# Output projection of eight row tiles: three of four partial products formed inside the attention loop and added to x by GpSimd

## The reference, cut to what matters

```python
def _L1_ffn_ref(x, pos_w, pos_b, qkv_w, qkv_b, wo_w, wo_b):      # HEADS 8, TOPK 16
    pos = lax.conv_general_dilated(...)                           # three taps along the rows
    x = x + (pos + pos_b[None, :, None]).transpose(0, 2, 1)
    qkv = x @ qkv_w.T + qkv_b
    q, k, v = jnp.split(qkv, [c, 2 * c], axis=-1)                 # then split into 8 heads of 64
    logits = jnp.einsum('bmd,bpd->bmp', qd * scale, kd)
    _, idx = lax.top_k(logits, TOPK)
    ...
    attn = jax.nn.softmax(jnp.einsum('bmd,bmkd->bmk', q * scale, k_sel), axis=-1)
    out = jnp.einsum('bmk,bmkd->bmd', attn, v_sel)
    ...
    return out @ wo_w.T + wo_b

x = x + _L1_ffn_ref(_layernorm(x, axis=-1)[None], ...)[0]
```

## Time and profile before

| | |
|---|---|
| median of 3 runs | 1774.48 us (1774.18 to 1774.99) |
| the profiled execution, own time | 1774.77 us |
| its span | 1772.1 us |
| TensorE matmuls busy | 1527.8 us, 86% |
| VectorE busy | 1062.0 us, 60% |
| ScalarE busy | 699.6 us, 39% |
| GpSimd busy | 525.6 us, 30% |
| mean granted TensorE clock | 0.965 of full speed |
| loop of the 80 turns (first maximum to last striking out) | 1234.7 to 1724.6 us |

### The profile page before, as it was taken

The page is one execution under the profiler, slowest core; times in us unless marked ns, Lnnn a source line. Parts: engine busy times, 40 slices in busy tenths (PEclk is TensorE's granted clock), DMA queues, the critical chain, the costliest instruction groups (busy, mean ns, idle before and its releaser), DMA issues. The chain is left out here.

```text
span 1772.1 us, 22747 instructions
## 1 busy us (share of the span) xinstructions
PE 1527.8 (86%) x8385; PEld 940.5 (53%) x8385; DVE 1062.0 (60%) x2052; ACT 699.6 (39%) x1333; POOL 525.6 (30%) x388
## 2 busy tenths in 40 slices
PE   1885888789787788999999989958898999998878
PEld 0332544344466665445454654535586676776654
DVE  4998433333478774111322331574999999999991
ACT  0224000133365554110111132042778778878771
POOL 0001100000456651000000006001876766676550
PEclk9998899899899999999999999989999999999999
DMA  6000100000622212300000020002011011111001
GB/s 220 1 1 1 74 0 0 0 1 1 179 60 43 48 31 86 132 0 0 1 0 0 1 72 0 0 1 60 1 31 31 1 31 31 23 32 31 1 1 58
DMA packets 28570, 56.99 MB, mean 32 GB/s; under 512 B 7904, under 2 KB 12644, under 8 KB 28208
## 3 DMA queue, kind: packets, MB, share of 16 engines
q1 hardware_dynamic: 27600, 54.01, 11.0%
q10 hardware_dynamic: 864, 1.57, 0.3%
HBM read 28.77 MB, written 5.84 MB: 20 GB/s over the span
## 5 line engine op out<-in xcount | busy, mean ns | idle before, releaser
L1431 POOL TENSOR_TENSOR tl_ex<-tl_ex,tl_left 128x1250 f32<-128x1250 f32 x80 | 209.8, 2622 | 37.3 <-ACT tl_left L1733 33.2
L1552 PE MATMUL tl_banks<-identf,tl_ex 128*128 128x128 f32 x800 | 139.4, 290 | 42.2 <-ACT tl_pt L1754 25.7
L1272 DVE SCALAR_TENSOR_TENSOR X<-ex_ps_x,g,X 128x512 f32<-128x512 f32 x80 | 59.9, 750 | 192.6 <-PE ex_ps_x L1165 192.6
L1138 PE MATMUL ex_ps_h<-yt,w 128*128 128x512 f32 (+1 forms) x384 | 144.5, 531 | 0.0
L1165 PE MATMUL ex_ps_x<-w,hid 128*128 128x512 f32 (+1 forms) x320 | 143.1, 599 | 0.0
L1552 PEld LDWEIGHTS tl_banks<-identf,tl_ex 128*128 128x128 f32 x800 | 90.0, 144 | 97.4 <-ACT tl_pt L1754 44.4
L1754 ACT COPY tl_pt<-tl_banks 128x512 f32<-128x512 f32 (+1 forms) x200 | 108.4, 542 | 83.5 <-PE tl_banks L1552 79.7
L1218 ACT ACTIVATE hid<-ex_ps_h,b 128x512 f32<-128x512 f32 (+1 forms) x48 | 29.2, 610 | 242.6 <-PE ex_ps_h L1138 242.6
L1829 DVE MAX8 tl_m<-tl_banks 128x8 f32<-128x1250 f32 x80 | 116.3, 1454 | 5.6 <-PE tl_banks L1529 5.6
L1733 ACT ACTIVATE tl_left<-tl_left,tl_negm 128x1250 f32<-128x1250 f32 x80 | 107.6, 1345 | 29.0 <-DVE tl_left L1837 28.6
L1835 DVE MAX8 tl_m<-tl_left 128x8 f32<-128x1250 f32 x80 | 117.1, 1464 | 2.8
(11 more groups left out here) (268 smaller groups left out, 2963.8 us busy)
## 6 DMA issues: line engine op xcount, KB each, us to landing
kl<-KT SPq DMA_DIRECT2D x16, 320.0 KB, 4.4
qs<-QO SPq DMA_DIRECT2D x16, 320.0 KB, 5.8
tl_kl<-tl_KT SPq DMA_DIRECT2D x16, 320.0 KB, 4.4
tl_qs<-tl_QO SPq DMA_DIRECT2D x16, 320.0 KB, 6.0
w<-in_L_ffn_W SPq DMA_DIRECT2D x8, 512.0 KB
w<-in_L_ffn_W SPq DMA_DIRECT2D x4, 1024.0 KB, 9.8
at_kept<-AT SPq DMA_DIRECT2D x1, 3200.0 KB, 9.0
AT<-at_kept SPq DMA_DIRECT2D x1, 3200.0 KB, 18.9
```

The lines of the kernel that those rows point to most:

```text
L1138: mm = pe.matmul(h_bank(u)[:, 0:w], w1[e][:, k, j * P:(j + 1) * P], yt[:, G % 2, k, 0:w], start=(k == 0), stop=(k == KD - 1))
L1431: pool.tensor_tensor(ex[:, n % EXS, 0:N], ex[:, n % EXS, 0:N], left[:, n % LEFT, :], ALU.subtract).then_inc(s_probs, 1)
L1552: mm = pe.transpose(ps_t[:, b * P:(b + 1) * P], ex[:, n % EXS, a + b * P:a + (b + 1) * P], m.identf[:, :])
```

## The change

The three first column blocks of QO are complete once the first six heads are done (turn 59, normalised by turn 63). For the first EARLY = 8 row tiles their three products with `wo` are formed as jobs `out` at turns 65, 67, ... 79, one row tile each; ScalarE copies the result into a new buffer `partial`, and GpSimd adds it to x two turns later. `project(t)` of these tiles then forms the product of the last block alone. So that `wo` is there in time, its transposes move from turns 61 to 67 to turns 57 to 63, and the raw weight is loaded at the start of the loop, by four DMAs, into four vectors (`bias0`, `bias1`, `gamma1`, `beta1`) that no one reads any more, since the old place was still in use.

```diff
+    EARLY = 8
     for b in range(KD):
-        work_at[61 + 2 * b] = ("wo", b, None)
+        work_at[57 + 2 * b] = ("wo", b, None)
+    for t in range(EARLY):
+        work_at[65 + 2 * t] = ("out", t, None)
...
-    qkv_jobs = jobs_before[61]
+    qkv_jobs = jobs_before[57]
...
-        raw_wo = space("tl_raw_wo", 40960, [P, KD, D])
+        raw_wo = (m.bias0, m.bias1, m.gamma1, m.beta1)
+        partial = space("tl_partial", 40960, [P, EARLY, D])
...
-                    if (i, half) == (3, 0):
-                        sp.wait_ge(s_job, qkv_jobs)
-                        sp.dma_start(raw_wo[:, :, :], rows_of(io["L1_ffn_wo_w"])).then_inc(s_wo_in, 16)
+                    if (i, half) == (0, 1):
+                        for b in range(KD):
+                            sp.dma_start(raw_wo[b][:, :], io["L1_ffn_wo_w"][b * P:(b + 1) * P, :]).then_inc(s_wo_in, 16)
...
+                if n - 2 in work_at and work_at[n - 2][0] == "out":
+                    t = work_at[n - 2][1]
+                    pool.wait_ge(s_job_kept, kept_after[n - 2])
+                    pool.tensor_tensor(m.X[:, t, :], m.X[:, t, :], partial[:, t, :], ALU.add).then_inc(s_added, 1)
+                    pool.wait_ge(s_added, t + 1)
...
+                    if kind == "out":
+                        pe.wait_ge(s_normed, (2 * HP - 3) * NT // 2 + i // 2 + 1)
...
+                    if part >= HP - 1:
+                        return
+                    mm = pe.matmul(ps_o, QO[:, part, i * P:(i + 1) * P], wo[:, part, :], start=(part == 0),
+                                   stop=(part == HP - 2))
...
-                for k in range(KD):
-                    mm = pe.matmul(proj_bank(t), QO[:, k, t * P:(t + 1) * P], wo[:, k, :], start=(k == 0),
+                ks = range(HP - 1, KD) if t < EARLY else range(KD)
+                for k in ks:
+                    mm = pe.matmul(proj_bank(t), QO[:, k, t * P:(t + 1) * P], wo[:, k, :], start=(k == ks[0]),
                                    stop=(k == KD - 1))
...
+                elif kind == "out":
+                    act.copy(partial[:, i, :], ps_o).then_inc(s_job_kept, 1)
                 else:
+                    act.wait_ge(s_job, qkv_jobs)
                     act.copy(wo[:, :, i * P:(i + 1) * P], ps_o.rearrange("p (k c) -> p k c", k=KD)
...
                 dve.wait_ge(s_biased, t + 1)
+                if t < EARLY:
+                    dve.wait_ge(s_added, t + 1)
                 dve.wait_ge(s_projected, t + 1)
```

More of the change, by code:

```diff
@@ L1321, in top_layer @@
         (s_zn, s_w_turned, s_w_kept, s_x_turned, s_x_kept, s_edge, s_tapped, s_mid, s_conv, s_first, s_first_kept,
-         s_job, s_job_kept, s_wo_in, s_staged_k,
+         s_job, s_job_kept, s_wo_in, s_added, s_staged_k,
          s_fetched_0, s_fetched_1, s_staged, s_scored, s_max, s_negm, s_read, s_max2, s_topped, s_exp, s_rest,
@@ L1325, in top_layer @@
          s_projected, s_final, s_stored) = s.signals(
-            "zn w_turned w_kept x_turned x_kept edge tapped mid conv first first_kept job job_kept wo_in staged_k "
+            "zn w_turned w_kept x_turned x_kept edge tapped mid conv first first_kept job job_kept wo_in added staged_k "
             "fetched_0 fetched_1 staged scored max negm read max2 topped exp rest sum inv blank probs turned kept "
@@ L1384, in _ @@
                                          ).then_inc(s_fetched[half], 16)
-                    if (i, half) == (3, 0):
-                        sp.wait_ge(s_job, qkv_jobs)
-                        sp.dma_start(raw_wo[:, :, :], rows_of(io["L1_ffn_wo_w"])).then_inc(s_wo_in, 16)
+                    if (i, half) == (0, 1):
+                        for b in range(KD):
+                            sp.dma_start(raw_wo[b][:, :], io["L1_ffn_wo_w"][b * P:(b + 1) * P, :]).then_inc(s_wo_in, 16)
             for half in range(2):
                 sp.wait_ge(s_fetched[half], 64 * HP)
-            sp.wait_ge(s_wo_in, 16)
+            sp.wait_ge(s_wo_in, 16 * KD)
             for t in range(NT):
@@ L1581, in job @@
                     if kind == "wo":
-                        pe.wait_ge(s_wo_in, 16)
+                        pe.wait_ge(s_wo_in, 16 * KD)
+                    if kind == "out":
+                        pe.wait_ge(s_normed, (2 * HP - 3) * NT // 2 + i // 2 + 1)
                 if kind == "qk":
@@ L1593, in job @@
                     mm = project_v(ps_o[:, (what[part] - what[0]) * P:], i, what[part:part + 1])
-                else:
-                    mm = pe.transpose(ps_o[:, part * P:(part + 1) * P], raw_wo[:, i, part * P:(part + 1) * P],
-                                      m.identf[:, :])
-                last = len(what) - 1 if kind == "v" else KD - 1
+                elif kind == "wo":
+                    mm = pe.transpose(ps_o[:, part * P:(part + 1) * P], raw_wo[i][:, part * P:(part + 1) * P],
+                                      m.identf[:, :])
+                else:
+                    if part >= HP - 1:
+                        return
+                    mm = pe.matmul(ps_o, QO[:, part, i * P:(i + 1) * P], wo[:, part, :], start=(part == 0),
+                                   stop=(part == HP - 2))
+                last = len(what) - 1 if kind == "v" else HP - 2 if kind == "out" else KD - 1
                 if part == last:
```

## The result

| | before | after |
|---|---|---|
| median beside each other, 4 runs each | 1774.74 us | 1759.84 us |
| their extremes | 1774.18 to 1776.22 | 1758.07 to 1761.30 |
| the profiled execution, own time | 1774.77 | 1758.07 |
| its span | 1772.1 | 1755.1 |
| first maximum of the loop, turn 0 | 1234.66 | 1234.47 |

The ratio is 0.9907, 95% interval 0.9891 to 0.9923: 14.9 us less by the medians, against 18.8 forecast. The median, 1759.84 us, is 4.1 above the 1755.7 of the forecast and inside its range. The loop from turn 0 to turn 79 takes 483.9 us in both. All of the gain lies behind the maximum of turn 79: 50.18 us from there to the last addition before, 33.28 after. I call this distance the tail; where the loop begins differs from execution to execution, the tail doesn't depend on that.

What follows compares the result with a forecast made beforehand. VectorE's searches were taken to bound the loop and TensorE the tail behind it. The terms -20.9, +2.0 and +0.1 sum to -18.8 us, giving 1755.7 us, with an 8-in-10 range of 1753.9 to 1761.

Steps and rivals of the forecast that it cites:

- (a): Tail projections: tiles 0 to 7 keep 16 of 64 matmuls; 20.9 us removed, all on the path.
- (c): Between tail projections: nothing removed, weighing waits for the copy of job 79; +0.1 us, bounds 0 and 0.6.
- (b): Out job of turn 79, directly before the tail: tail starts later, +2.0 us, bounds 0.9 and 3.5.
- (d): Tile 8's round trip through ScalarE and GpSimd: 1.51 us, covered by 1.74 us of matmuls; bounds 0 and +0.5 us.
- (e): The other out jobs, in the loop: 2.6 us of TensorE every other turn, hidden by VectorE; 0.
- (f): Output weight transposes moved to turns 57 to 63, behind the V jobs: 0, bounds 0 and 1.2 us.
- (h): Output weight's 1 MB load moved to four DMAs at the start: hidden by some 57 turns, 0.
- (i): Tail: VectorE's and SyncE's added waits are met long before; the end stays 3.5 us behind the last matmul.
- (g): GpSimd's eight additions of partial tiles to x, turns 67 to 81: 0, bounds 0 and 0.2 us.
- rival C: Port lock: eight additions each hold VectorE 1.27 us, +10.2 us, 1765.9 us; chance 0.07 with the way to it.
- Rival A: TensorE's clock falls to half in the tail: 1757.2 to 1758.7 us; beyond 1758.5, chance 0.17 shared with B.
- B: Small stalls in loop and tail, 1 to 4 us together: 1757 to 1760 us; beyond 1758.5, chance 0.17 shared with Rival A.

Runs made afterwards that it cites:

- `adds4`: The changed kernel with a second GpSimd addition of the same size after each of the seven in the loop; 1756.69 us median, ratio 0.9889.
- the jobs alone: The changed kernel with out jobs and copies kept but their results unused, every tile projected in full; 1779.0 us median, ratio 1.0010 to the kernel before.
- the other order: The changed kernel with tiles 0 to 2 projected between the last transposes, tile 3 before the last weighing, the rest behind; 1754.72 us median.
- all ten tiles: Against the changed kernel: ten out jobs at turns 59 to 77, output weight transposed at turns 17 to 39, projections reordered; 1748.11 us median, ratio 0.9836.

## Why the prediction was right, and where it was off

The mechanism was as forecast: the matmuls taken from the tail are the gain, and the loop hides seven of the eight jobs. At full clock the tail is 31.64 us where the forecast had 31.4 (50.18 less 18.8): 18.5 us gained against 18.8. By the steps:

- (a) and (c): from the first projection to the last addition 45.7 us before and 1745.79 - 1720.77 = 25.0 after at full clock (`adds4`), 20.7 less; forecast 20.9 - 0.1. The waiting of the second weighing for job 79's copy didn't show: 4.72 us from 1726.76 to 1731.48, as before.
- (b): +2.16 us against +2.0. The choice of turn 27 as the nearest row was right; the bounds of 0.9 and 3.5 weren't needed.
- (d): tile 8's input was ready at 1743.54 + 0.73 = 1744.27, and the four matmuls in front of it end 1.74 us after 1742.75, at 1744.49. The cover held, and barely: TensorE's weight load for tile 8 waited 0.42 us for GpSimd, and still the block of 20 matmuls took 8.85 us, as 20 of the 32 do before (14.00 for 32, 7.13 for 16). The round trip that does bite is another, ScalarE's exponential of turn 79, and with eight jobs it is covered.
- (e): turns 65 to 75 took 1694.32 - 1634.07 = 60.25 us, forecast 60.2. No reciprocal waited after turn 57.
- (f), (h): nothing, by the kernel without out jobs, 50.17 us of tail and 483.97 of loop. (i): nothing, by the changed kernel's own profile, where the last matmul ends at 1751.60 and the span 3.5 us later, as before.
- (g): nothing, by the doubled additions. The Trainium skill (SBUF — State Buffer, section on SBUF's two separate sides) has a lock only for VectorE instructions in a 2-port mode or with two SBUF inputs. The prediction let it reach each of VectorE's passes, and its rows don't say that: a maximum reads one tensor, and a striking out lists `tl_m` beside the other, eight values that an instruction of its own (MATCH_VALUE_LOAD) loads. No hold shows beside these passes, with 15 additions as with 8; whether the lock's condition was ever met here no run shows, so rival C was tested and the page's rule was not.
- Rival A came in where the forecast said full clock: the step that failed is "the clock at 1.00 from 1724 on". One fall, 1.64 us, stands in each of the three profiles of the changed kernel (I had up to 1.5). The reasons on both sides were weak. "The tail of now has those stops too and no fall" is true of the row and says little: the tail of the jobs alone has its fall behind the same stops between the same long blocks. "More of the tail is waits" doesn't carry it either, for the tails with four and with seven jobs have the short blocks and more waiting, and no fall. The Trainium skill (TensorE: Matmul & The Clock Gate, Part 1) has the clock follow how busy TensorE was lately. The traces agree in part: each fall stands directly behind a stretch with 2.05 of 3.40 us busy. But the same stretch has no fall behind it in other executions, and just behind the maximum of turn 79 TensorE does less still (0.74 us busy of 3.40 before, 1.52 in the changed kernel), with the granted clock at 1.00 there and next behind it.
- The half clock stretches that left the loop were worth nothing, as (e) implied.

In the first comparison the profiled executions differ by 1774.77 - 1758.07 = 16.7 us, the 18.5 less the fall's 1.64 to within 0.2. The medians differ by 14.9 there and by 16.3 and 19.7 in the two comparisons that hold the same tail again (1759.62 against 1775.94, 1756.69 against 1776.40). The rest lies in the spread of the runs. I had allowed half a microsecond for it, from three runs within 0.8 us; with 17 runs the same kernel covers 12 us. So of the 4.1 us that the median lies above the forecast, 1.64 are the fall, if the timed runs have it as the profiles do, 0.2 the sizes of the terms, and some 2.2 the spread. That the range held them is partly luck: it reached to 1761 for rivals A and B, and not for this.

The place of the spread is ahead of the loop: over the 13 profiled executions the loop begins anywhere in 10.6 us, and time less loop start, loop and tail is 5.1 to 6.4 us in all. The clock goes with it: the mean granted clock was 0.970 in the execution that began the loop at 1230.16 and 0.964 in the one at 1240.80, and 0.968 and 0.959 in the fastest and the slowest of 17 runs of the kernel before (1770.89 and 1781.47 us). That half clock stretches alone make the spread was not tried.

## What to carry to other kernels

Work at the end of a program that needs only part of the last results can be cut along the sum and its early part given to an engine that waits in the loop before: here seven of the eight jobs with their copies and additions vanished beside VectorE, and only the one next to the end cost anything, 2.2 us. Find the nearest job of the same kind that the loop already hides, and read from its rows what the new one will do, the end of its turn included. A tail made of short blocks should have its independent pieces set into the waits, and its gain read against a mark inside the program, since the time of the whole spreads over 12 us, more than any term here but (a) is worth.

## What was not expected of the hardware

TensorE did the same in two tails, busy for 2.05 of 3.40 us in both, and in one the granted clock fell to 0.51 for 3.4 us while in the other it stayed at 1.00. Nine of the 13 profiled tails hold such a stretch, and four of the nine have a fall directly behind it: the changed kernel's, three of three (33.28, 33.29 and 33.28 us against 31.64 without), and that of the jobs alone, in a tail of long blocks (8.83 us for a block of 7.13). The other five are those of the kernel before, of the doubled additions, and of no, four and seven jobs. The four tails whose waits are filled or used (filled waits twice, the other order, all ten tiles) hold no stretch as empty behind the first projection (2.25 us busy of 3.40 at the least, in that of all ten tiles) and have no fall. This speaks for filling the waits, and is too little to show it.
